# The iterative inverse carries 8 columns of N·V instead of a 64-column matrix

## The chip, the cores and the metric

The kernel runs on one core of a Trainium2 chip. The metric is the device time of one execution in microseconds (us); the time before is the median of three runs. A core has TensorE (PE in the profile, its weight loads PEld), VectorE (DVE), ScalarE (ACT), GpSimd (POOL) and SyncE (SP, the DMA queue).

## The reference, cut to what matters

The program computes two transformer-like layers over x of shape (4, 1024, 128). The change lies in the attention of layer 1, with 16 heads of 8 columns and 64 landmarks, and touches the counting of the mixture-of-experts router:

```python
def _iterative_inv(K, n_iter=6):
    I = jnp.eye(K.shape[-1], dtype=K.dtype)
    denom = jnp.max(jnp.sum(K, axis=-2), axis=-1)[..., None, None]
    V = K.swapaxes(-1, -2) / denom
    for _ in range(n_iter):
        KV = K @ V
        V = 0.25 * V @ (13.0 * I - KV @ (15.0 * I - KV @ (7.0 * I - KV)))
    return V
...
L = softmax(q @ k_l.T)            # (T, 64) of each head
P = _iterative_inv(softmax(q_l @ k_l.T))   # (64, 64)
N = softmax(q_l @ k.T)            # (64, T)
y = L @ (P @ (N @ v))             # N @ v: 64 x 8
...
oh = jax.nn.one_hot(e_ord, E)     # 2 * 4096 entries, 8 experts
cnt = take_along_axis(cumsum(oh, 0) - oh, e_ord[:, None], 1)[:, 0]
```

There are 4 x 16 = 64 heads, kept as 32 pairs: head 0 of a pair on partitions 0 to 63, head 1 on 64 to 127.

## The kernel before, in words

The program is a row of blocks, with all engines meeting between two of them: inputs of layer 0, its attention (the long part, up to about 850 us), its outputs (`layer0_outputs`), `inverse_and_routing`, `layer1_attention`, `experts`, `combine`. Within a block each engine has its own instruction list, in order, and waits on semaphores.

`layer0_outputs` loops over the four batches and leaves, for `inverse_and_routing`: KS (K after its softmax, 128 x 32 pairs x 64), NV (N·v, 128 x 32 x 8), and `oh`, the one-hot choices of the router (128 x 512). Its last instructions of a batch are the transposes of nvT on TensorE (L1207), the scaling of NV and `k_softmax` on VectorE (L968 to L971). Its GpSimd list also makes `upper` and `ones`, the left operands of the two counting products.

`inverse_and_routing` (from 987.4 us to 1098.5 us of the profiled execution) keeps A = K·V of each iteration in the left 64 columns of AQ, and Q, the product of the factors so far, in its right 64 columns. The 32 pairs are handled in NG = 4 groups of GR = 8 pairs. `squared(n, ...)` issues the products of a group: 8 pairs times 2 halves, 16 matmuls of 64 x 64 weights in fp32, each two records in the trace. A group's result of 64 columns fills one PSUM bank. TensorE's order (L1434 is the line of all of these, since the helper records them):

1. two counting products into banks 7 and 6 (L1445, L1446);
2. four column sums of K into banks 0 to 3 (L1450);
3. K transposed, four groups in banks 4 and 5 in turn, copied to X by ScalarE (L1406);
4. the Gram products K^T against itself, which give A up to the factor 1/denom;
5. six iterations of three passes of four groups: A times (7 - A), A times X, and X times AQ (128 columns, two banks a group), which gives the next A and Q at once. In the last iteration the third pass makes only Q (64 columns);
6. Q times NV (8 columns), then K^T times z (8 columns).

VectorE takes the maximum of the column sums (L1370, one instruction over four banks), its reciprocal, fills the right half of AQ with the identity over denom (L1373, 128 x 2048), scales the Gram products (L1377) and forms 7 - A (L1380); in the loop it forms 15 - and 13 - the product out of PSUM (L1387) and 7 - A of the next iteration (L1394). Between these lie small instructions for the next block: `landmarks` (L1345) and 32 memsets of `sums` (L1354). ScalarE copies the counts (L1402), the transposed K, the third pass times 0.25 (L1411, in the last iteration L1413), z (L1417), and the blocks of WM (L1426, four instructions a group).

GpSimd clears WM and `spread` and marks `spread` (L1299 to L1304), then runs the routing chain on the counts (L1311 to L1333), marks the entries and sends 32 batches of rows by indirect DMA (L1261). Each of these waits for a certain number of the groups of TensorE's loop (`i_mm`), so that they are spread over it:

```python
pool.wait_ge(sem("i_mm"), AHEAD + t * (MM * ITERS - AHEAD) // NT)   # AHEAD 12, MM 12, ITERS 6, NT 32
```

At its end GpSimd waits until all have landed.

## Time and profile before

| | us |
|---|---|
| median of three runs (lowest, highest) | 1415.3 (1413.99, 1415.97) |
| the profiled execution's own time | 1400.87 |
| its span in the trace | 1399.1 |
| TensorE busy in the span | 1265.2 (90%) |
| VectorE busy | 1009.8 (72%) |
| ScalarE busy | 864.0 (62%) |
| GpSimd busy | 236.2 (17%) |
| mean granted TensorE clock | 0.954 |

Busy shares are averages over stages with different limits; which engine sets the pace of a stage is read from that stage's rows. A granted clock of 1.00 is 2.4 GHz, 0.50 is 1.2 GHz. A name like L1434 is a line of the kernel. The instruction's line of a helper stands for all its calls, so these are told apart by the tiles and shapes behind it.

### The profile page before, as it was taken

The page shows a single profiled execution, that of the slowest core. Times are in us where ns is not written, and L with a number is a line of the kernel's source. Part 1 is how long each engine was busy: PE and PEld are TensorE (multiplying, and loading weights), DVE is VectorE, ACT ScalarE, POOL GpSimd, SP SyncE. Part 2 cuts the span into 40 slices and gives each one's busy share as a digit, 9 for nine tenths or more (in the row PEclk, how much of TensorE's full clock was granted, in tenths as well). Part 3 has the DMA queues.
Part 4 walks back from the last instruction along what each step waited for, and adds up shares of the span by engine and source line. Part 5 has one row for each costly group of instructions (what it writes and reads, how often), then busy time and mean ns, then how long its engine had stood idle before and what let it go on. Part 6 is the DMA issues. An engine that isn't in the chain of part 4 may idle for free. (4 is left out here: it accounts for less than half of the span.)

```text
span 1399.1 us, 26250 instructions
## 1 busy us (share of the span) xinstructions
PE 1265.2 (90%) x10433; PEld 595.5 (43%) x10433; DVE 1009.8 (72%) x1309; ACT 864.0 (62%) x1459; POOL 236.2 (17%) x306
## 2 busy tenths in 40 slices
PE   6967999999999999999999988898899899999990
PEld 4631222222222222222222235555699666678870
DVE  6877888898998988899899637665756388623324
ACT  3533878788887787888888855555132466543331
POOL 4200110000000000000000011100644222125560
PEclk9976999999999999999999989999999699999995
DMA  4763133331334323322120021100001111123316
GB/s 145 214 189 67 32 67 84 71 71 47 67 86 98 108 78 72 67 62 48 27 64 10 6 55 33 46 16 15 18 28 34 59 35 43 47 65 99 100 57 186
DMA packets 75206, 94.98 MB, mean 68 GB/s; under 512 B 13236, under 2 KB 44684, under 8 KB 74052
## 3 DMA queue, kind: packets, MB, share of 16 engines
q1 hardware_dynamic: 69996, 83.19, 23.6%
q0 software_dynamic: 5088, 10.12, 2.3%
q8 instruction: 82, 1.34, 0.4%
q14 instruction: 40, 0.33, 0.1%
HBM read 54.30 MB, written 38.56 MB: 66 GB/s over the span
## 5 line engine op out<-in xcount | busy, mean ns | idle before, releaser
L664 ACT ACTIVATE b_exp_ring<-psum 128x512 f32<-128x512 f32 x1024 | 555.5, 599 | 158.2 <-PE psum L719 155.0
L606 DVE TENSOR_REDUCE b_mx<-psum 128x2 f32<-128x1024 f32 x507 | 595.8, 1219 | 75.9 <-PE psum L551 74.8
L719 PE MATMUL psum<-b_q,b_k 75*128 75x512 bf16 x1024 | 311.9, 387 | 10.7 <-DMA b_q<-b_neg 9.1
L695 PE MATMUL psum<-b_exp_ring,b_v 128*32 128x512 f32 x2048 | 274.5, 608 | 0.9 <-ACT b_exp_ring L664 0.7
L719 PEld LDWEIGHTS psum<-b_q,b_k 75*128 75x128 bf16 x1024 | 79.2, 97 | 328.4 <-ACT b_exp_ring L664 223.6
L550 PE MATMUL psum<-b_k,b_q 64*128 64x512 bf16 x512 | 169.0, 395 | 25.4 <-DVE b_mx L606 10.5
L551 PE MATMUL psum<-b_ko,b_qo 64*128 64x512 bf16 x512 | 169.0, 395 | 0.0
L734 POOL CAST b_neg<-b_neg_rest 16x128 bf16<-16x128 f32 x32 | 8.9, 280 | 661.4 <-DVE b_neg_rest L617 661.4
L1835 ACT ACTIVATE e_hT<-psum,e_b 128x358 f32<-128x358 f32 (+3 forms) x96 | 53.7, 560 | 75.6 <-PE psum L1855 72.3
L550 PEld LDWEIGHTS psum<-b_k,b_q 64*128 64x128 bf16 x512 | 44.1, 93 | 127.5 <-DVE b_mx L606 41.8
L695 PEld LDWEIGHTS psum<-b_exp_ring,b_v 128*32 128x32 f32 x2048 | 41.2, 108 | 108.2 <-issue 106.4
L1261 POOL DMA_INDIRECT x_disp<-x_norm,row_sent x64 | 62.5, 976 | 122.1 <-PE psum L1633 81.4
L1765 POOL DMA_INDIRECT y_tok<-e_y,e_dest x72 | 70.8, 984 | 70.7 <-DVE e_y L1807 51.5
L1865 PE MATMUL psum<-e_w,e_hT 128*128 128x128 f32 (+1 forms) x576 | 67.4, 277 | 0.0
L1569 DVE TENSOR_REDUCE f_max<-psum 128x16 f32<-128x1024 f32 x32 | 39.2, 1225 | 37.3 <-PE psum L1633 36.5
L1865 PEld LDWEIGHTS psum<-e_w,e_hT 128*128 128x128 f32 (+1 forms) x576 | 64.6, 184 | 1.8
L1613 ACT ACTIVATE f_le<-f_lx 128x1024 f32<-128x1024 f32 x32 | 33.8, 1057 | 47.3 <-DVE f_lx L1575 47.3
L1855 PE MATMUL psum<-e_xT,e_w 128*128 128x358 f32 (+3 forms) x192 | 60.2, 468 | 0.9 <-DVE e_xT L1779 0.9
L991 DVE TENSOR_REDUCE c_nm<-psum 128x1 f32<-128x1024 f32 x32 | 37.7, 1220 | 31.7 <-PE psum L1148 31.6
L1411 ACT ACTIVATE i_aq<-psum 128x1024 f32<-128x1024 f32 x20 | 20.5, 1024 | 58.7 <-PE psum L1434 58.7
L1095 ACT ACTIVATE c_en<-psum,c_nm 128x1024 f32<-128x1024 f32 x32 | 35.7, 1117 | 32.1 <-DVE c_nm L991 32.1
L1434 PE MATMUL psum<-i_x,i_aq 64*64 64x64 f32 x1536 | 46.2, 218 | 1.4 <-DVE i_x L1380 1.4
(281 smaller groups left out, 1487.4 us busy)
## 6 DMA issues: line engine op xcount, KB each, us to landing
b_q<-q_ops SPq DMA_DIRECT2D x48, 192.0 KB
b_k<-k_ops SPq DMA_DIRECT2D x48, 192.0 KB
k_ops<-a_k SPq DMA_DIRECT2D x20, 256.0 KB, 3.2
x_disp<-b_zeros SPq DMA_DIRECT2D x13, 320.0 KB
e_x<-x_disp SPq DMA_DIRECT2D x8, 520.0 KB
v_ops<-a_vs SPq DMA_DIRECT2D x4, 1024.0 KB, 5.1
b_v<-v_ops SPq DMA_DIRECT2D x16, 256.0 KB
av_out<-b_acc SPq DMA_DIRECT2D x128, 32.0 KB, 1.7
```

What stands on the lines that cost most here:

```text
L550: g.nc.tensor.matmul(g.bank(2 * (n % 2)), q[0:MROWS, 2 * p, t], k[0:MROWS, 2 * p, keys], start=True, stop=True)
L551: return g.nc.tensor.matmul(g.bank(2 * (n % 2) + 1), qo[MROWS:P, p, t], ko[MROWS:P, p, keys], start=True, stop=True)
L606: nc.vector.reduce_max(mx[:, d % 2, :, i // 2, i % 2], pair, AX.X).then_inc(sem("b_max_done"), 1)
L664: act.activation(ex[:, n % E_RING, :], g.bank(5 + n % 3), ACT.Exp, scale=ATT_SCALE)\
L695: last = nc.tensor.matmul(AV[32 * i:32 * i + 32, :], v[s][:, at_v:at_v + 32], ex[:, (4 * group + i) % E_RING, :], start=(kb == 0), stop=(k ...
L719: nc.tensor.matmul(g.bank(5 + n % 3), k[s][0:XROWS, h, kb * P:(kb + 1) * P], q[s][0:XROWS, h, half * BANK:(half + 1) * BANK], start=True, ...
L1261: pool.indirect_dma_start(g.x_disp[:, :], bass.IndirectOffsetOnAxis(g.rows_out[:, n:n + 1], 0), g.XNW[:, n % NT, :], None).then_inc(g.sem( ...
L1434: last = nc.tensor.matmul(out[half, i, :], lhs(n * GR + i, half), rhs(n * GR + i, half), start=True, stop=True)
L1765: pool.indirect_dma_start(g.y_tok[:, :], bass.IndirectOffsetOnAxis(dest[c][0:r, t:t + 1], 0), y[c][0:r, t, :], None).then_inc(sem(f"e_sent ...
L1835: act.activation(hT[c][:, i, lo:hi], g.ps[:, (3 + n % 3) * BANK:(3 + n % 3) * BANK + hi - lo], ACT.Gelu, bias=b1[c][:, i:i + 1]).then_inc( ...
L1855: nc.tensor.matmul(g.ps[:, (3 + n % 3) * BANK:(3 + n % 3) * BANK + hi - lo], w1[c][:, i * P:(i + 1) * P], xT[:, lo:hi], start=True, stop=T ...
L1865: last = nc.tensor.matmul(g.ps[0:r, col:col + D], hT[c][:, i, t * P:t * P + r], w2[c][:, i, :], start=(i == 0), stop=(i == HC - 1))
```

## The change

It does six things. (1) Q is gone: a tile AZ holds A (64 columns) and Z (8 columns) of each pair. Z starts as NV times 1/denom, and every iteration multiplies it by its factor; the third pass has 72 columns, in the last iteration 8. All factors are polynomials in one matrix, so their order is free. The product with NV at the end is gone. (2) The two counting products move to the end of `layer0_outputs`, into banks 2 and 3, and the copies of the counts wait for nothing. (3) K's transposes come first, in four banks of their own, then the column sums; VectorE takes maximum and reciprocal for each group of pairs as its column sum comes. (4) The fills of WM, `spread` and `sums` go behind the routing chain on GpSimd, the ones in `sums` as two selections in place of 32 memsets on VectorE. (5) The dispatches' waits are spread over five iterations in place of six. (6) The blocks of WM are copied out half on ScalarE, half on VectorE.

```diff
# layer0_outputs, TensorE, after the last batch
+            chosen = g.oh[:, :, :, :].rearrange("p k n e -> p (k n e)")
+            pe.wait_ge(sem("c_kx"), B)
+            nc.tensor.matmul(g.bank(COUNTS), g.upper[:, :], chosen, start=True, stop=True).then_inc(sem("r_counts"), 1)
+            nc.tensor.matmul(g.bank(COUNTS + 1), g.ones[:, :], chosen, start=True, stop=True).then_inc(sem("r_counts"), 1)
...
# inverse_and_routing
+    ZW = LM + HD
+        AZ = sb("i_az", [P, NPAIR, ZW])
-        AQ = sb("i_aq", [P, NPAIR, P])
...
+    def landmark_block(eng_op, n, i, name):
+        w = narrow(2 * n + 1).rearrange("p (j r) d -> p j r d", r=2)
+        wm = grp(g.WM, n).rearrange("p (j r) c -> p j r c", r=2)
+        for r in range(2):
+            c = 16 * r + HD * i
+            eng_op(wm[halves[i], :, r, c:c + HD], w[halves[i], :, r, :]).then_inc(g.sem(name), 1)
...
# GpSimd: the fills stand behind the routing chain
-            nc.gpsimd.memset(g.WM[:, :, :], 0.0).then_inc(sem("i_wm"), 1)
-            nc.gpsimd.memset(g.spread[:, :, :], 0.0).then_inc(sem("f_spread"), 1)
...
+            nc.gpsimd.memset(g.WM[:, :, :], 0.0).then_inc(sem("i_wm_clear"), 1)
+            nc.gpsimd.memset(g.spread[:, :, :], 0.0).then_inc(sem("f_spread"), 1)
+            nc.gpsimd.memset(g.sums[:, :, :, :], 0.0).then_inc(sem("f_sums"), 1)
...
+            for i, half in enumerate(halves):
+                pool.wait_ge(sem("f_sums"), 1 + i)
+                to = g.sums[half, :, :, :].rearrange("p s r (t c) -> p (s r) t c", t=2)
+                nc.gpsimd.affine_select(out=to, in_=to, compare_op=ALU.not_equal, fill=1.0, base=-i,
+                                        pattern=[[-2, 2 * STEPS], [0, 2], [1, 16]], channel_multiplier=0)\
+                  .then_inc(sem("f_sums"), 1)
...
-                pool.wait_ge(sem("i_mm"), AHEAD + t * (MM * ITERS - AHEAD) // NT)
+                pool.wait_ge(sem("i_mm"), AHEAD + t * (PR * (ITERS - 1) - AHEAD) // NT)
...
# VectorE
-            link(nc.vector.reduce_max(den[:, :], g.bank(0, 4).rearrange("p (n c) -> p n c", c=LM), AX.X))
-            nc.vector.reciprocal(den[:, :], den[:, :]).then_inc(sem("i_den"), 1)
-            dve.wait_ge(sem("i_den"), 1)
-            nc.vector.tensor_tensor(AQ[:, :, LM:P], eyes[:, 3, :].unsqueeze(1).broadcast_to([P, NPAIR, LM]),
-                                    over_last(den[:, :], LM), ALU.mult).then_inc(sem("i_den"), 1)
+            for n in range(NG):
+                mine = slice(n * GR, (n + 1) * GR)
+                dve.wait_ge(sem("i_colsum"), n + 1)
+                nc.vector.reduce_max(den[:, mine], squares(n), AX.X).then_inc(sem("i_den"), 1)
+                dve.wait_ge(sem("i_den"), 2 * n + 1)
+                nc.vector.reciprocal(den[:, mine], den[:, mine]).then_inc(sem("i_den"), 1)
+            dve.wait_ge(sem("i_den"), 2 * NG)
+            nc.vector.tensor_tensor(AZ[:, :, LM:ZW], g.NV[:, :, :], over_last(den[:, :], HD), ALU.mult)\
+              .then_inc(sem("i_z0"), 1)
...
+            for n in range(NG):
+                dve.wait_ge(sem("i_landmark"), n + 1)
+                landmark_block(nc.vector.tensor_copy, n, 1, "i_wm_low")
...
# ScalarE
-                        act.activation(grp(AQ, n), both_banks(n), ACT.Copy, scale=0.25).then_inc(sem("i_aq"), 1)
+                        act.activation(grp(AZ, n), pairs_of(n)[:, :, 0:ZW], ACT.Copy, scale=0.25).then_inc(sem("i_az"), 1)
...
+                        act.activation(grp(z, n), pairs_of(n)[:, :, LM:ZW], ACT.Copy, scale=0.25).then_inc(sem("i_az"), 1)
...
# TensorE
-            nc.tensor.matmul(g.bank(7), g.upper[:, :], both, start=True, stop=True).then_inc(sem("r_counts"), 1)
-            nc.tensor.matmul(g.bank(6), g.ones[:, :], both, start=True, stop=True).then_inc(sem("r_counts"), 1)
...
+            for n in range(NG):
+                products(n, squares(4 + n), k_of, lambda p, half: g.ident[half, half], "i_kt_ps")
...
+                if n == COUNTS:
+                    pe.wait_ge(sem("r_counted"), 3)
+                nc.tensor.matmul(g.bank(n), twin[:, :], grp(g.KS, n).rearrange("p n c -> p (n c)"), start=True, stop=True)\
+                  .then_inc(sem("i_colsum"), 1)
...
+            pe.wait_ge(sem("i_z0"), 1)
...
+                cols = slice(LM if it + 1 == ITERS else 0, ZW)
                 for n in range(NG):
-                    pe.wait_ge(sem("i_x"), at(it, XS, 2 * NG + n + 1))
-                    if it + 1 < ITERS:
-                        squared(n, both_banks(n), x_of, aq_of, "i_mm")
-                    else:
-                        squared(n, both_banks(n)[:, :, LM:P], x_of, q_of, "i_mm")
+                    pe.wait_ge(sem("i_x"), at(it, PR, 2 * NG + n + 1))
+                    products(n, pairs_of(n)[:, :, cols], x_of, lambda p, half: AZ[half, p, cols], "i_mm")
             for n in range(NG):
-                pe.wait_ge(sem("i_aq"), at(ITERS - 1, AC, n + 1))
-                squared(n, narrow(2 * n), q_of, lambda p, half: g.NV[half, p, :], "i_z")
-            for n in range(NG):
-                pe.wait_ge(sem("i_z_out"), n + 1)
-                squared(n, narrow(2 * n + 1), lambda p, half: g.KS[half, p, :], lambda p, half: z[half, p, :], "i_w")
+                pe.wait_ge(sem("i_az"), at(ITERS - 1, NG, n + 1))
+                products(n, narrow(2 * n + 1), k_of, lambda p, half: z[half, p, :], "i_landmark")
```

`products` is `squared` under a new name, `pairs_of` is `both_banks`, `k_of` reads KS.

## Rows read from the trace of the kernel before

**Rows 1.** The page, its first part: busy us, share and instructions.

```profile
PE 1265.2 (90%) x10433; PEld 595.5 (43%) x10433; DVE 1009.8 (72%) x1309; ACT 864.0 (62%) x1459; POOL 236.2 (17%) x306
```

**Rows 2.** Windows: length, busy PE, PEld, DVE, ACT, POOL; clock, DMA, GB/s.

```profile
1026.60:1041.00 14.40, 14.40 (x390) 14.40 (x386) 8.43 (x22) 4.10 (x4) 6.76 (x7) 1.00 0.10 32
...
1098.50:1125.00 26.50, 20.51 (x108) 13.12 (x112) 16.32 (x20) 11.01 (x11) 7.69 (x11) 0.51 0.23 70
```

**Rows 3.** Timeline, one iteration: start, us, engine, line, what [idle before].

```profile
1012.23 7.16 PE L1434 MATMUL psum<-i_aq,i_x 64*64 64x128 f32 x128
...
1014.19 1.02 ACT L1411 ACTIVATE i_aq<-psum 128x1024 f32<-128x1024 f32 x1 [15.11 <-PE psum L1434]
...
1019.22 7.63 PE L1434 MATMUL psum<-i_x,i_aq 64*64 64x64 f32 x256
...
1026.68 7.16 PE L1434 MATMUL psum<-i_aq,i_x 64*64 64x128 f32 x128
```

**Rows 4.** Timeline, the block's start.

```profile
986.45 0.69 DVE L971 TENSOR_TENSOR k_softmax<-c_ke,c_small 128x512 f32<-128x512 f32 x1
...
987.47 1.54 PE L1445 MATMUL psum<-r_onehot,r_upper 128*128 128x512 f32 x2 [2.96 <-PEq L904]
...
990.51 4.04 PE L1450 MATMUL psum<-k_softmax,i_ones 128*128 128x512 f32 x8
...
992.25 0.19 PEld L1450 LDWEIGHTS psum<-k_softmax,i_ones 128*128 128x128 f32 x1 [0.24 <-issue]
...
994.66 2.29 DVE L1370 TENSOR_REDUCE i_den<-psum 128x32 f32<-128x2048 f32 x1 [3.66 <-PE psum L1450]
...
1000.36 0.69 DVE L1377 TENSOR_TENSOR i_aq<-psum,i_den 128x512 f32<-128x512 f32 x1
...
1006.42 1.04 DVE L1380 SCALAR_TENSOR_TENSOR i_x<-i_aq,i_eyes 128x512 f32<-128x512 f32 x1
...
1007.51 4.88 PE L1434 MATMUL psum<-i_x,i_aq 64*64 64x64 f32 x160 [0.53 <-DVE i_x L1380]
```

**Rows 5.** Timeline, the block's end.

```profile
1088.23 3.85 PE L1434 MATMUL psum<-nv,i_aq 64*64 64x8 f32 x128
...
1089.33 0.22 ACT L1417 ACTIVATE i_z<-psum 128x64 f32<-128x64 f32 x1 [0.29 <-PE psum L1434]
...
1091.93 5.45 PE L1434 MATMUL psum<-i_z,k_softmax 64*64 64x8 f32 x128
...
1097.42 0.84 ACT L1426 ACTIVATE w_landmark<-psum 64x32 f32<-64x32 f32 x4 [0.87 <-PE psum L1434]
...
1098.53 0.35 POOL L1535 MEMSET e_x<- 128x130 f32 x2 [10.75 <-POOLq L1294]
```

**Rows 6.** Groups in the block, VectorE and GpSimd: busy us, mean ns | idle before.

```profile
L1394 DVE SCALAR_TENSOR_TENSOR i_x<-i_aq,i_eyes 128x512 f32<-128x512 f32 x20 | 13.8, 692 | 24.6 <-ACT i_aq L1411 24.6
L1380 DVE SCALAR_TENSOR_TENSOR i_x<-i_aq,i_eyes 128x512 f32<-128x512 f32 x4 | 4.5, 1116 | 0.1
...
L1345 DVE SCALAR_TENSOR_TENSOR f_klm<-kl_sums,mask 128x256 f32<-128x256 f32 x4 | 1.7, 416 | 0.0
...
L1304 POOL TENSOR_SCALAR_AFFINE_SELECT f_spread<-f_spread 128x128 f32<-128x128 f32 x4 | 1.5, 410 | 0.2 <-POOL f_spread L1300 0.2
```

**Rows 7.** Timeline of GpSimd: routing chain and dispatch.

```profile
992.41 1.25 POOL L1311 TENSOR_TENSOR r_tot<-r_tot 128x504 f32<-128x504 f32 x1 [1.89 <-ACT r_tot L1402]
...
1015.12 0.24 POOL L1256 COPY x_norm<-choice_weight 128x32 f32<-128x32 f32 x1
...
1021.73 0.96 POOL L1261 DMA_INDIRECT x_disp<-x_norm,row_sent  x1 [0.30 <-issue]
```

**Rows 8.** Windows of 2 us; the clock is the third number from the right.

```profile
988.00:990.00 2.00, 2.00 (x4) 0.96 (x3) 1.74 (x7) 0.00 (x0) 1.84 (x5) 0.50 0.78 235
...
1092.00:1094.00 2.00, 2.00 (x72) 2.00 (x70) 0.00 (x0) 0.99 (x5) 0.00 (x0) 0.95 0.03 8
1094.00:1096.00 2.00, 2.00 (x42) 2.00 (x42) 0.00 (x0) 1.03 (x6) 0.00 (x0) 0.50 0.01 4
```

More of the change, by code:

```diff
@@ L158 @@
 ITERS = 6
+COUNTS = 2
 AHEAD = 12
@@ L1298, in _ @@
             link = Link(pool, sem("pool_step"), start=g.pool_steps)
-            nc.gpsimd.memset(g.WM[:, :, :], 0.0).then_inc(sem("i_wm"), 1)
-            nc.gpsimd.memset(g.spread[:, :, :], 0.0).then_inc(sem("f_spread"), 1)
-            pool.wait_ge(sem("f_spread"), 1)
-            for s in range(STEPS):
-                to = g.spread[:, s, :].rearrange("p (j h d) -> p j h d", j=4, h=HQ)
-                nc.gpsimd.affine_select(out=to, in_=to, compare_op=ALU.not_equal, fill=1.0, base=-HQ * s,
-                                        pattern=[[-32, 4], [-1, HQ], [0, HD]], channel_multiplier=1)\
-                  .then_inc(sem("f_spread"), 1)
             pool.wait_ge(sem("r_counted"), 3)
@@ L1347, in landmarks, with first @@
                   .then_inc(sem("f_klm"), 1)
-            def ones_of(s):
-                for r in range(2):
-                    for i in range(2):
-                        row = HQ * s + 2 * r + i
-                        for c in (row, 16 + row):
-                            nc.vector.memset(g.sums[LM * i:LM * i + LM, s, r, c:c + 1], 1.0).then_inc(sem("f_sums"), 1)
-            nc.vector.memset(g.sums[:, :, :, :], 0.0).then_inc(sem("f_sums"), 1)
+            def first(n):
+                nc.vector.scalar_tensor_tensor(grp(X, n), grp(AZ, n)[:, :, 0:LM], -1.0, eye(0), ALU.mult, ALU.add)\
+                  .then_inc(sem("i_x"), 1)
             nc.vector.memset(twin[:, :], 0.0).then_inc(sem("i_twin"), 1)
             dve.wait_ge(sem("i_twin"), 1)
-            dve.wait_ge(sem("f_sums"), 1)
             for half in halves:
                 nc.vector.memset(twin[half, half], 1.0).then_inc(sem("i_twin"), 1)
-            for i, f in enumerate((7.0, 15.0, 13.0, 1.0)):
+            for i, f in enumerate((7.0, 15.0, 13.0)):
                 for half in halves:
@@ L1378, in _ @@
                                         ALU.mult).then_inc(sem("i_a"), 1)
                 dve.wait_ge(sem("i_a"), n + 1)
-                nc.vector.scalar_tensor_tensor(grp(X, n), grp(AQ, n)[:, :, 0:LM], -1.0, eye(0), ALU.mult, ALU.add)\
-                  .then_inc(sem("i_x"), 1)
-            g.dve_steps = link.n
-            for it in range(0, ITERS):
+                first(n)
+            for it in range(ITERS):
                 for stage in range(2):
                     for n in range(NG):
-                        dve.wait_ge(sem("i_mm"), at(it, MM, stage * NG + n + 1))
+                        dve.wait_ge(sem("i_mm"), at(it, PR, stage * NG + n + 1))
@@ L1387, in _ @@
                         nc.vector.scalar_tensor_tensor(grp(X, n), squares(2 * n + stage), -1.0, eye(1 + stage),
                                                        ALU.mult, ALU.add).then_inc(sem("i_x"), 1)
[L1389 to L1390 removed]
+                if it < B:
+                    landmarks(it)
                 for n in range(NG if it + 1 < ITERS else 0):
[L1393 to L1395 removed]
+                    dve.wait_ge(sem("i_az"), at(it, NG, n + 1))
+                    first(n)
```

80 lines of the change are left out of this document (29 added, 51 removed).

## The prediction

> **What bounds the kernel now.** I read the page's first part, the busy shares, first: TensorE is busy 90% of the span [rows 1]. That is an average, so I went to the stretches of the block that the diff edits. In the middle of the loop TensorE is busy for all of a stretch of 14.4 us, at the full granted clock, while VectorE is busy 8.4 us and ScalarE 4.1 us of it [rows 2]. The reader is to see that TensorE alone paces the loop. The timeline of one iteration says what it pays for: four groups of the 128-column product start at 1012.23, the eight groups of 64-column products at 1019.22, the next 128-column ones at 1026.68 [rows 3]. So a 128-column group costs (1019.22 - 1012.23) / 4 = 1.747 us, a 64-column group (1026.68 - 1019.22) / 8 = 0.932 us, an iteration 14.45 us.
>
> The block's start is another stage. TensorE does counts (987.47), column sums (990.51), transposes of K and Gram products, but the first products of the loop have to wait for VectorE, which goes from the reduction (994.66) over its fill of AQ and the scaling that starts at 1000.36 to the fourth X, done at 1007.46; TensorE starts the last group of the first product at 1007.51 [rows 4]. The start is VectorE's, 20.0 us from 987.47 to 1007.51. The end of the block is a chain again: the NV product 1088.23, the K product 1091.93 to 1097.38, four ScalarE copies from 1097.42 to 1098.26 [rows 5], and the next block begins at once behind them.
>
> **The change, part by part.**
>
> *Loop, 128 to 72 columns.* Rows exist for 128 columns (1.747 us), for 64 (0.932) and for 8: the NV product's four groups take 1091.93 - 1088.23 = 3.70 us, 0.925 each [rows 5]. That 8 columns cost what 64 do says that a floor (32 weight loads and 32 matmul records a group) lies near 0.93, and that 128 columns are paced by the columns. In proportion to columns, 72 cost 1.747 x 72/128 = 0.983 us. Bounds: the floor, 0.932; and the straight line between the rows of 64 and 128, 1.034. I take 0.983, since 72 is just over the point where columns and floor meet (68). Four groups: 3.93 in place of 6.99 us, 3.06 less, five times: **15.3 us** (14.3 to 16.3). The last iteration's product goes from 64 to 8 columns, which by the rows above gives nothing.
> Cover: a group's way round is its 0.98, ScalarE's copy of 576 elements (on the line between 0.22 for 64 and 1.02 for 1024 [rows 3, 5], 0.65), VectorE's 0.69 [rows 6] and some 0.3 of handover, 2.6 us, against 4.9 us until TensorE needs that group again. VectorE needs 12 x 0.69 + 0.42 = 8.7 of 11.4 us. So TensorE stays the bound; the landmark fills (0.42 [rows 6]) and the freed 32 small memsets lie under it.
>
> *NV stage removed.* Z is carried along, so the four groups at 1088.23 go, and with them ScalarE's copies of z from their place between two products: **3.7 us**. The copy of Z group n after the last iteration (64 elements, 0.22 us [rows 5]) lies under groups n+1 to 3, and the K product of group 0 can follow on directly.
>
> *Copies of the landmark blocks.* Four ScalarE copies at the end (0.84 us [rows 5]) become two on ScalarE beside two on VectorE, which has nothing to do there: **0.4 us** (0 to 0.6). K products themselves: 5.45 us, of which the clock's part is below.
>
> *Block's start.* The two counting products (from 987.47 to the column sums at 990.51, 3.0 us) move into the outputs' end. There TensorE is done at 984.51 (987.47 less its 2.96 us of idleness) and VectorE works to 987.14 [rows 4]; at the full clock the two cost four records of 0.43 (a column sum's weight load of 0.19 behind 0.24 of idleness, at the full clock [rows 4]), 1.7 us, so they end at 986.3 and VectorE still ends the block. At half clock it would be 3.4 us, ending at 988.0: up to 0.9 us lost. I take 0. Then the new order: K transposes from 987.47, four groups of 64 columns, 3.73 [rows 3]; column sums, eight records, 3.4, to 994.6. ScalarE copies the counts meanwhile (three copies of 512 elements, 0.6 each by the line above, done by 989.3) and frees the two banks long before column sum 2. VectorE reduces each group as it comes, so only the last reduction is left (512 elements, 0.69 as the multiplication of that size at 986.45 [rows 4]), a reciprocal (0.2, an estimate: the smallest instructions here take 0.22 [rows 5]), and Z0 over 256 elements, 0.42 by the landmark fill of that size [rows 6], 0.3 more for handovers: ready at 996.2. Before, it came to this point at 1000.36. The first Gram product (from 994.6, 0.93) lies ahead of it. Then the same eight VectorE instructions as before, which took 1000.36 to 1007.46, 7.1 us: fourth X at 1003.3, last group starts at 1003.4. **4.1 us** less.
> Bounds: the X instructions took 1.12 us here and 0.69 in the loop, with the same shape [rows 6]; GpSimd was in its routing chain beside the former, and only sent rows beside the latter. The chain will start about 3 us earlier (its first instruction is at 992.41, released by the copies of the counts, its last at 1015.12 [rows 7]) but with 23 us it still covers 996 to 1003, so I keep 1.12. Without that neighbour four instructions would save 1.7 more: 5.8. Below: if the clock is low for the first 3.5 us, as it was at 988 to 990 [rows 8], two groups at double price are 1.8 us lost: 2.3.
> The Trainium skill, "SBUF — State Buffer", section "SBUF: two separate sides", says that VectorE (with two SBUF inputs) and a GpSimd instruction that reads SBUF lock each other out of a shared port pair for a whole instruction. The rows agree, since the subtraction of AQ and eyes reads SBUF twice (1.12), while the scaling out of PSUM stays at 0.69. By that rule Z0, with two SBUF inputs, may wait a GpSimd instruction as well, and the sum would be about 1 us less.
>
> *GpSimd.* The fills of WM, spread and sums move behind the routing chain: three memsets and six selections, of which four take 0.41 for 128 elements [rows 6]; the others are of 256 to 1,024 elements, and I count 0.7 for each of those five, 5 us in all (an estimate). Chain from 989.3 plus 23.0 plus 5: dispatches start at 1017.3. They are 32, at 0.96 + 0.30 = 1.26 us back to back [rows 7], so 1058. The waits now want product 58 at the latest, which is at about 1056. The block will end near 1075, and DMA landing has 17 us. Before, GpSimd sat 10.75 us between its last dispatch and the next block [rows 5]. Cost 0; the cover is those 17 us. SP's queue: the two query loads keep their place.
>
> Sum: 15.3 + 3.7 + 0.4 + 4.1 = **23.5 us**. The profiled execution took 1400.9 us (span 1399.1), the median of the runs is 1415.3, so 14.4 us lie between an execution with and without the profiler; I carry the difference over unchanged: 1415.3 - 23.5 = **1391.8 us** (profiled: 1377.4).
>
> **The clock.** TensorE's granted clock is 1.00 (2.4 GHz) up to 1092, 0.95 in the next 2 us and 0.50 (1.2 GHz) from 1094 [rows 8], in the middle of products of 8 columns that came without a gap; it stays there to about 1125 in the next block [rows 2]. In the changed kernel the run of 8-column products is as long (last iteration's in place of NV's, then K's), so I leave the fall where it is. If it doesn't come, the K products cost 3.7, and 1.7 us are won; in the next block's low stretch TensorE is busy 20.5 of 26.5 us [rows 2], and a fall or rise that comes some us sooner or later moves the time by part of that; I allow 2 us either way for it.
> The Trainium skill, "TensorE: Matmul & The Clock Gate", section "What's actually happening", has the clock fall to half after idleness. The rows show it falling while TensorE is recorded as busy all the time, so for this place I go by the rows. By the page there would be no fall here, and the gain would be 25.2 us.
>
> **Rivals.**
> (a) *Clock falls inside the loop* (ends slower). 8 columns brought it down [rows 8]; the loop now carries fewer columns. Against it: eight groups of 64 columns, 7.46 us in a row, five times, leave it at 1.00 [rows 2, 3], and 72 is more than 64. Price: groups double at most, 0.93 to 1.86; it decides from 24 us of the 65 us loop on; all of it low would be 65 - 23.5 = 42 us slower, 1457. Chance 4%.
> (b) *The way round, not TensorE, sets the loop*: GpSimd's fills and dispatches slow VectorE's X (1.12 for 0.69), or a wide group waits for its bank. The three VectorE passes of an iteration would need 12 x 1.12 = 13.4 us, 2 us over 11.4, but GpSimd's SBUF-reading work ends with the second iteration and eight of the twelve read PSUM: at most 2 iterations, 4 us lost: 1396. If it held throughout, 10 us lost: 1402. Chance 10% for 1396 to 1405.
> (c) *Gain stays, routing now ends the block*: it decides from 17 us on by which GpSimd or its DMAs end later than I think, and 40 us later the gain is all gone: 1415. Nothing speaks for it but the missing landing times. Chance 3%.
> (d) *Forecast*, 83%, of it (e) low clock at the block's start, 1.8 us less, 1393.6, a third.
>
> **How the numbers follow.** The bounds add to 14.3 + 3.7 + 0 + 2.3 - 0.9 = 19.4 and 16.3 + 3.7 + 0.6 + 5.8 + 1.7 = 28.1 us, with the next block's clock a few us more on either side: 1385 to 1398 holds the forecast and the nearer half of (b). Faster by over 0.2% (2.8 us, about what a measurement of this kernel can tell): 0.83 + 0.10 = 0.93; within: 0.03 from (c); slower: 0.04 from (a).
>
> **What the profile will show.** The 72-column groups start 0.98 us apart, and iterations 11.4 us (0.93 and 11.2, or 1.03 and 11.6, are my bounds). The first loop product's last group starts 15.9 us behind the block's start. No product reads NV in this block. VectorE's X of the first pass costs 1.1 us each. GpSimd's dispatches run back to back and end about 17 us ahead of the block. A PEclk row under 0.9 between the first and last 72-column product, a VectorE wait that TensorE sits behind in later iterations, or an outputs' block that ends later than VectorE's last multiplication would make me wrong.

## The result, and the profile after

The changed kernel takes 1403.7 us (median of 4 runs, 1401.9 to 1405.3), the kernel before 1415.6 beside it (4 runs, 1414.0 to 1418.0): ratio 0.9922, 95% interval 0.9901 to 0.9943. It is faster, by 11.9 us where 23.5 were forecast, and its time is 5.7 us above the range of 1385 to 1398. The profiled execution took 1402.7 us, its span 1400.7: no 14 us lie between the two this time.

The page's first part answers to [rows 1]. TensorE is recorded as busy 5.8 us less, where 15.3 + 3.7 us of its work were to go:

```profile
PE 1259.4 (90%) x10305; PEld 584.6 (42%) x10305; DVE 1008.6 (72%) x1288; ACT 851.2 (61%) x1447; POOL 236.5 (17%) x309
```

The windows next, one iteration in the middle of the loop and then the last one (columns as in [rows 2]):

```profile
1046.30:1061.10 14.80, 13.36 (x384) 12.37 (x385) 8.38 (x13) 2.49 (x4) 7.88 (x8) 1.00 0.13 39
...
1076.20:1087.35 11.15, 11.15 (x390) 11.15 (x387) 6.64 (x10) 1.65 (x5) 0.00 (x0) 1.00 0.02 7
```

An iteration was to take 11.4 us and takes 14.8. In [rows 2] TensorE was busy for 14.40 of 14.40 us; here it is idle for 1.44 of 14.80, at the full clock. In the last iteration, where GpSimd does nothing (0.00), TensorE is busy throughout, and does as many matmuls (390) in 11.15 us as in the middle (384) in 14.80. So the loss is larger than the recorded idleness. The waits between 1031 and 1076 us (who, for whom: us in total, times, longest) say what the idleness waits for:

```profile
POOL x_disp L1266 <- PE psum L1442: 21.6, 25, 1.2
DVE i_x L1404 <- PE psum L1442: 13.2, 15, 1.0
PEld psum L1442 <- issue: 7.1, 18, 0.5
...
PE psum L1442 <- issue: 4.5, 13, 0.4
```

In the last two rows TensorE waits for nothing that the profile shows ("issue"); no engine's result is what it lacks. I read this as instructions that come late, which is an argument so far. VectorE and GpSimd wait for TensorE, not the reverse. The timeline shows beside what:

```profile
1018.41 1.15 POOL L1266 DMA_INDIRECT x_disp<-x_norm,row_sent  x1 [0.57 <-POOL x_norm L1261]
...
1019.87 0.96 POOL L1266 DMA_INDIRECT x_disp<-x_norm,row_sent  x1 [0.30 <-issue]
1020.40 0.39 PE L1442 MATMUL psum<-i_x,i_az 64*64 64x64 f32 x6 [0.33 <-issue]
...
1021.13 0.36 PE L1442 MATMUL psum<-i_x,i_az 64*64 64x64 f32 x5 [0.34 <-issue]
1021.14 0.96 POOL L1266 DMA_INDIRECT x_disp<-x_norm,row_sent  x1 [0.30 <-issue]
...
1035.22 3.35 PE L1442 MATMUL psum<-i_x,i_az 64*64 64x64 f32 x97 [0.39 <-issue]
...
1036.00 0.96 POOL L1266 DMA_INDIRECT x_disp<-x_norm,row_sent  x1 [1.16 <-PE psum L1442]
...
1076.21 7.66 PE L1442 MATMUL psum<-i_x,i_az 64*64 64x64 f32 x256
...
1083.67 3.88 PE L1442 MATMUL psum<-i_az,i_x 64*64 64x8 f32 x128
...
1087.38 5.84 PE L1442 MATMUL psum<-i_z,k_softmax 64*64 64x8 f32 x128
...
1093.84 0.35 POOL L1526 MEMSET e_x<- 128x130 f32 x2 [18.29 <-POOLq L1308]
```

TensorE runs in short pieces of 5 or 6 matmuls while GpSimd sends rows back to back, and in unbroken stretches of 128 and 256 once the sends are over. The last row but one is K's product, the last GpSimd's first work in the next block.

The block's start, also from the timeline, beside [rows 4]:

```profile
987.29 1.02 PE L1218 MATMUL psum<-r_onehot,r_ones 128*128 128x512 f32 x2
988.54 0.69 DVE L972 TENSOR_TENSOR k_softmax<-c_ke,c_small 128x512 f32<-128x512 f32 x1
989.56 3.95 PE L1442 MATMUL psum<-ident,k_softmax 64*64 64x64 f32 x128 [1.24 <-PEq L905]
...
993.43 3.70 PE L1456 MATMUL psum<-k_softmax,i_ones 128*128 128x512 f32 x8
...
998.14 0.55 DVE L1391 TENSOR_TENSOR i_az<-nv,i_den 128x256 f32<-128x256 f32 x1
...
1004.65 1.05 DVE L1373 SCALAR_TENSOR_TENSOR i_x<-i_az,i_eyes 128x512 f32<-128x512 f32 x1
1005.75 4.88 PE L1442 MATMUL psum<-i_x,i_az 64*64 64x64 f32 x160 [0.53 <-DVE i_x L1373]
```

The counting products end at 988.31, before VectorE's last multiplication does (989.23). Counted from the K transposes (989.56), the column sums end after 7.6 us (forecast 7.1), Z0 is ready after 9.1 (8.7), and the last group starts after 16.2 (15.9).

The traces are compared below by five stages, cut at VectorE's instructions: *start* (from the memset of i_ones, with which the block begins, to the end of the fourth X), *loop* (from the start of the first X multiplication that reads a product to that of the last, 48 of them), *tail* (from there to the first maximum of attention, f_max), *attention* (first to last of its 32 maxima), and *rest* (to the end of the span).

| us | start | loop | tail | attention | rest |
|---|---|---|---|---|---|
| before, the trace of the rows | 19.7 | 77.3 | 15.4 | 110.3 | 188.7 |
| changed | 16.1 | 78.3 | 11.5 | 112.4 | 192.9 |

Read so, the loop has got longer, and so have two stages that the diff doesn't touch. That was the first riddle.

### The profile page after: what moved, and what is told of

Read it like the earlier page. It is cut to its first block and busy times, and to the rows that moved or that the text cites. A ratio compares the mean times of both kernels' runs of the same rounds, so it can differ in the third digit from the quotient of the medians.

```text
span 1400.7 us, 25966 instructions
## 1 busy us (share of the span) xinstructions
PE 1259.4 (90%) x10305; PEld 584.6 (42%) x10305; DVE 1008.6 (72%) x1288; ACT 851.2 (61%) x1447; POOL 236.5 (17%) x309
## 3 DMA queue, kind: packets, MB, share of 16 engines
q1 hardware_dynamic: 69996, 83.19, 23.4%
## 5 line engine op out<-in xcount | busy, mean ns | idle before, releaser
L1442 PE MATMUL psum<-i_x,i_az 64*64 64x64 f32 x1536 | 53.1, 222 | 6.3 <-issue 4.5
L1428 ACT ACTIVATE i_az<-psum 128x576 f32<-128x576 f32 x20 | 12.6, 650 | 70.5 <-PE psum L1442 70.5
## 6 DMA issues: line engine op xcount, KB each, us to landing
b_q<-q_ops SPq DMA_DIRECT2D x48, 192.0 KB
b_k<-k_ops SPq DMA_DIRECT2D x48, 192.0 KB
```

The source lines that it names most:

```text
L1442: last = nc.tensor.matmul(out[half, i, :], lhs(n * GR + i, half), rhs(n * GR + i, half), start=True, stop=True)
```

## Experiments

Eighteen runs were made, in six sessions, each session on one chip with the kernel before beside it; the first and the fourth fell on the same chip, so five chips took part. Theory S ("theory A" in the expectations): GpSimd's indirect sends hold up TensorE's supply of instructions, and narrow products leave no reserve against that. Rivals: W, it is GpSimd's waits for TensorE's products; D, it is the data that the sends move; N (near "theory B"), the 72-column form is itself slower than I forecast. A last one, I, stands in the expectation of a2: the 16 KB loads of instructions cause the gaps.

### First session: kernel before; padded; sends moved

*a0* is the kernel before. *a1* pads the passes of 72 columns to 128 with zeros:

```diff
-        AZ = sb("i_az", [P, NPAIR, ZW])
+        AZ = sb("i_az", [P, NPAIR, P])
...
+            nc.gpsimd.memset(AZ[:, :, ZW:P], 0.0).then_inc(sem("i_pad"), 1)
...
-                cols = slice(LM if it + 1 == ITERS else 0, ZW)
+                cols = slice(LM, ZW) if it + 1 == ITERS else slice(0, P)
```

*a2* sends nothing in the loop, and two blocks of 128 rows in each tile of attention (the marking of the entries moves to the middle of attention with them):

```diff
-            for t in range(NT):
-                pool.wait_ge(sem("i_mm"), AHEAD + t * (PR * (ITERS - 1) - AHEAD) // NT)
-                dispatch(g, pool, t)
-            pool.wait_ge(sem("dispatched"), 16 * NT)
...
             for n in range(NT):
                 pool.wait_ge(sem("f_scores"), n + 1)
-                dispatch(g, pool, NT + n)
+                dispatch(g, pool, 2 * n)
+                dispatch(g, pool, 2 * n + 1)
```

*a3* is a2 with the 32 waits kept, each before a memset of one column in place of the send.

> The kernel before, unchanged, profiled beside the others, because its profiled execution of the first session took 1400.9 us and its timed runs 1414 to 1418. If the two belong to two chips or sessions, this execution takes about 1415 us and its trace says which block has the 14 us. If the profiler makes it faster, it takes 1401 again. In the block of the inverse both theories expect iterations of 14.45 us and no gap over 0.1 us in TensorE's starts of 64-column products.

> The changed kernel with a third pass of 128 columns again (56 of them zeros; ScalarE still copies 72, Z still has 8). Theory A, TensorE's instruction supply: a 64-column group uses its instructions as fast as they come (29 ns each), each indirect send of GpSimd holds the supply up for about half a microsecond, and the wide pass used to let the queue fill again. Then iterations with sends take 14.45 us here, no longer than the 14.75 us of the changed kernel, with no gaps, and the whole is within 3 us of the changed kernel, rather faster. Theory B, columns: the gaps of the changed kernel have another cause (the fills of GpSimd, the layout of AZ), which stays, and 3.06 us a pass come on top: iterations of 17.8 us, 15 us slower.

> The changed kernel with all 64 sends in the attention block, two a tile, none in the loop. Theory A: all five iterations take 11.2 to 11.4 us as the last one does, the loop is 17 to 20 us shorter, the attention block gets some us longer if the sends hold TensorE up there too; net 10 to 19 us faster than the changed kernel, about 1388. Theory B: the gaps stay, nothing is gained. A third theory, instruction loads: the 16 KB loads alone cause the gaps; they stay too.

> As a2_sends_in_attention, but GpSimd keeps the 32 waits on the loop's products, with a memset of one column behind each in place of the send. If the send itself holds up TensorE (theory A), iterations take 11.2 to 11.4 us as in a2. If it is the waiting on TensorE's semaphore, they take 14.7 us as in the changed kernel.

Measured: the kernel before took 1399.8 us here, not 1415 (13 runs); a0 1401.8 (ratio 1.0003, 0.9984 to 1.0022), a1 1392.1 (0.9934, 0.9910 to 0.9957), a2 1376.9 (0.9833, 0.9805 to 0.9861), a3 1379.7 (0.9850, 0.9817 to 0.9883). a0's profiled execution took 1406.0 us with a span of 1404.2. So an execution with the profiler isn't 14 us shorter than one without: there are chips on which the kernel before takes 1400 us, and others on which it takes 1415. The trace of the rows came from one of the former, the timed runs from one of the latter. On this chip iterations of 128 columns took 14.45 us with the sends in them, as in the rows, and a2's and a3's 11.47. The 14.45 us that I had expected of a1 came, and of a2 and a3 about the 11.2 to 11.4. But nothing held TensorE up here, so a1 to a3 can't tell S, W and D apart.

### Second session: changed again; before again; before with sends moved; 96 columns

*b0* is the changed kernel, *b1* the one before. *b2* is the kernel before with a2's edit; *b3* is a1 with 96 in place of 128.

> The changed kernel, unchanged, beside the others. Its first profile had iterations of 14.7 us with gaps in TensorE's starts and 3.54 us a tile in the attention, where every other trace has 3.45; the kernel before was timed at 1415 in that session and at 1400 in the last one. If theory A holds for the kernel (narrow passes leave no reserve, each send costs 0.41 us), the gaps are here again and it is about 16 us slower than the version with the sends in the attention, 1390 to 1393 if before is at 1400. If the gaps belonged to that session's chip, iterations take 11.5 us here and it is at 1376 to 1380.

> The kernel before, once more, for its trace on the chip of these runs: 14.45 us an iteration, 3.45 us a tile, 1397 to 1406 in all if the chip is like the last one. What differs between executions should lie ahead of the changed block.

> The kernel before with all 64 sends in the attention block. Theory A: its wide passes hid the sends already, so its iterations stay at 14.45 us and the whole stays within 2 us. So the gain of the changed kernel with the same move would be the change's own, not the move's. If the sends cost TensorE time in the kernel before too, this one is some us faster.

> The changed kernel with a third pass of 96 columns (24 of them zeros). Columns alone: 4 x 1.747 x 96/128 = 5.24 and 7.46 for the other two passes, 12.7 us an iteration. Theory A in numbers: supply for an iteration takes 12 x 0.93 = 11.2 us, eight sends 8 x 0.41 = 3.3 us, 14.5 us together, whichever is more: so 14.5 to 14.75 us again, and a time within 2 us of the changed kernel.

Measured, with the kernel before at 1413.4 us (19 runs): b0 1399.6 (0.9900, 0.9884 to 0.9917), b1 1415.0 (1.0002, 0.9987 to 1.0018), b2 1413.8 (1.0004, 0.9990 to 1.0019), b3 1402.6 (0.9918, 0.9899 to 0.9937). The windows show that the kernel before is held up on this chip too; b1, the same length in the middle of the loop:

```profile
1040.00:1054.80 14.80, 14.38 (x354) 13.84 (x349) 7.77 (x20) 4.10 (x4) 5.76 (x6) 1.00 0.10 30
```

TensorE is idle 0.42 us there, where [rows 2] has none, and it gets through fewer matmuls: 354 in 14.8 us, against 390 in 14.4. b1's loop is 82.9 us. Without sends (b2) it is back at 77.3, and attention grows from 112.9 to 118.4, so the time stays. I had expected b1 like the first session's chip (14.45 us an iteration; it has about 15.5), b3's iterations at 14.5 to 14.75 us and its time within 2 us of b0's. They are 15.35 us and it is 3.0 us slower: the padding isn't free, and a sum of a fixed price a send on top of a floor doesn't give it.

### Third session: changed; sends moved; plain copies; sends later

*c0* is the changed kernel, *c1* is a2. *c2* leaves the first 32 indirect sends out, so half the routed rows never arrive; SyncE copies the same rows to a spare place in DRAM, behind the same products:

```diff
+            for t in range(NT):
+                sp.wait_ge(sem("i_mm"), AHEAD + t * (PR * (ITERS - 1) - AHEAD) // NT)
+                sp.dma_start(spare_rows[t, :, :], g.XNW[:, t, :]).then_inc(sem("plain"), 16)
```

*c3* sends later, over the whole loop:

```diff
-                pool.wait_ge(sem("i_mm"), AHEAD + t * (PR * (ITERS - 1) - AHEAD) // NT)
+                pool.wait_ge(sem("i_mm"), 20 + t * (PR * ITERS - 20) // NT)
```

> So far the kernel before ran at 1400 with no gaps and 3.45 us a tile of the attention on some chips (kind I: its first profile, the four kernels of the first call), and at 1414 with gaps at the sends and 3.54 us a tile on others (kind II: its first timed runs, the changed kernel's two profiles, the second call). If this call falls on kind I (before near 1400), theory A with the kinds expects iterations of 11.47 us, no gaps, and 1376 to 1379, the forecast's 23 us. If on kind II (before near 1414), again 14.7 us an iteration and 1399 to 1404. A theory in which the sends cost TensorE time in this kernel on every chip expects gaps on kind I too.

> The changed kernel with all sends in the attention, two a tile, which had 11.47 us an iteration and 3.45 us a tile on kind I. On kind II: iterations of 11.47 us (16 us less than the changed kernel there) but tiles of 3.85 us in place of 3.54 (31 tiles, 9.6 us more), so 5 to 8 us faster than the changed kernel. On kind I: the same time as the changed kernel within 2 us.

> The first 32 indirect sends of GpSimd are left out (half of the routed rows never arrive), and SyncE copies as many rows of the same size to a spare place in their stead, at the same products of the loop. On kind II: if it is the data moved that holds TensorE up, the gaps and the 14.7 us stay; if it is GpSimd's making of the descriptors, iterations take 11.5 us. On kind I no gaps in either.

> The changed kernel with the sends from product 20 on and spread to the end of the sixth iteration, 1.6 products apart, so that GpSimd never has three to catch up with. On kind II: no run of gaps at the start, the clock stays at 1.00, the first full iteration loses its extra 3 us and the sum of the others stays (32 times 0.4 us): 2 to 4 us faster than the changed kernel. On kind I no difference.

Measured, before at 1413.7 us (7 runs): c0 1399.7 (0.9897, 0.9877 to 0.9916), c1 1392.8 (0.9857, 0.9832 to 0.9882), c2 1383.8 (two runs; 0.9786, 0.9761 to 0.9812), c3 1399.4 (0.9903, 0.9881 to 0.9925). The windows of the same 14.8 us in the middle of the loop, for c0:

```profile
1040.00:1054.80 14.80, 13.17 (x383) 12.12 (x380) 8.24 (x13) 2.49 (x4) 7.88 (x8) 1.00 0.13 38
```

for c1:

```profile
1040.00:1054.80 14.80, 14.80 (x498) 14.80 (x496) 10.24 (x17) 3.91 (x6) 0.00 (x0) 1.00 0.02 4
```

and for c2:

```profile
1040.00:1054.80 14.80, 14.80 (x501) 14.80 (x498) 10.31 (x17) 3.26 (x5) 0.00 (x0) 1.00 0.18 50
```

With the eight sends (c0) TensorE does 383 matmuls and is idle 1.63 us; without them about 500 and is never idle. c2 moves more data than c0 in this stretch (50 GB/s against 38), and nothing is lost: theory D falls, and N with it, since c1's and c2's iterations are 11.47 us on this chip as well. Theory I falls too: the loops of c0, c1 and d0 have 17 loads of instructions each, and only c0's has gaps.

The gaps also lie at a fixed distance from the send. The last send of c0's loop, and TensorE's next weight load behind a gap:

```profile
1074.05 0.96 POOL L1266 DMA_INDIRECT x_disp<-x_norm,row_sent  x1 [0.72 <-PE psum L1442]
...
1075.41 0.26 PEld L1442 LDWEIGHTS psum<-i_az,i_x 64*64 64x64 f32 x6 [0.51 <-issue]
```

The load starts 1.36 us behind the send's start. For all of the last 26 sends of this loop it is 1.31 to 1.39 us, though GpSimd waited 0.5 to 1.5 us before them, and no product is waited for behind the last one. This speaks against W, as do the two sends at 1019.87 and 1021.14 in the profile after, which waited for no product ("issue") and have the densest gaps. The tiles of attention's maxima in c1 show where a part of the gain goes back:

```profile
L1559 DVE TENSOR_REDUCE f_max<-psum x32: 1224/1225/1226, 1075.2 to 1194.8; 128x16 f32<-128x1024 f32 x32
```

and in c0:

```profile
L1560 DVE TENSOR_REDUCE f_max<-psum x32: 1224/1225/1226, 1095.9 to 1206.4; 128x16 f32<-128x1024 f32 x32
```

119.6 us with two sends a tile, 110.5 with one: 9.1 us for 32 sends, 0.28 each; by b1 and b2 it was 5.5 us, 0.17 each. Both kernels have the same wait per tile there, so in attention it is the second send and not the wait. (On the first session's chip the same edit takes attention from 109.3, d0 below, to 109.8.) c3 was to be 2 to 4 us faster than c0 and is 0.3. Its clock stays at 1.00 in the loop, as expected, and its loop is 4.3 us shorter than c0's (75.0), but its tail is 1.9 and its attention 2.5 longer: next to nothing is won.

### Fourth session: changed; 128 columns

*d0* is the changed kernel and *d1* is a1.

> The changed kernel once more, to catch a chip of kind I. If before is near 1400 (kind I): 11.47 us an iteration, no gaps, 3.45 us a tile, 1375 to 1380 by theory A with kinds; 1386 or more and gaps if narrow passes make the sends costly on every chip. If before is near 1414 (kind II): 14.7 to 15.1 us, as in three profiles so far.

> The changed kernel with a third pass of 128 columns, which on kind I took 14.45 us an iteration with no gaps and told nothing of the sends. On kind II: the kernel before takes 15.5 us an iteration there with 6.4 sends, the pass of 96 columns 15.35 with 8. If width only buys reserve against the sends: 15.4 to 15.9 us, within 6 us of the changed kernel (15 by columns alone). On kind I: as before, 1390 to 1393.

It ran on the chip of the first session. Before took 1402.1 us (12 runs), d0 1378.7 (0.9829, 0.9800 to 0.9858), d1 1395.4 (0.9946, 0.9925 to 0.9968). Here the changed kernel, with the same sends behind the same products, gains what was forecast: 23.4 us. (d1 was expected at 1390 to 1393 and is 2 us above; a1, the same kernel on this chip, took 1392.1.) d0's window of 14.8 us in the loop:

```profile
1040.00:1054.80 14.80, 14.80 (x505) 14.80 (x503) 11.18 (x18) 3.31 (x6) 11.45 (x12) 1.00 0.17 54
```

Twelve sends (GpSimd busy 11.45 us) and TensorE never idle. Its timeline, a send in the middle of an unbroken stretch of 128 matmuls:

```profile
1024.71 4.17 PE L1442 MATMUL psum<-i_az,i_x 64*64 64x72 f32 x128
...
1025.19 0.96 POOL L1266 DMA_INDIRECT x_disp<-x_norm,row_sent  x1 [0.30 <-PE psum L1442]
...
1028.71 3.49 PE L1442 MATMUL psum<-i_x,i_az 64*64 64x64 f32 x114
```

### Fifth session: 128 columns; half the sends

*e0* is a1 again, *e1* keeps 16 of the 32 sends in the loop, three products apart, and puts 48 into attention:

```diff
-            for t in range(NT):
-                pool.wait_ge(sem("i_mm"), AHEAD + t * (PR * (ITERS - 1) - AHEAD) // NT)
+            for t in range(NT // 2):
+                pool.wait_ge(sem("i_mm"), AHEAD + 2 * t * (PR * (ITERS - 1) - AHEAD) // NT)
                 dispatch(g, pool, t)
```

> The changed kernel with a third pass of 128 columns, third try for a chip of kind II (before near 1414). There: 15.4 to 15.9 us an iteration, since the kernel before takes 15.5 with 6.4 sends an iteration and this one has 8; the loop no more than 3 to 6 us longer than the changed kernel's 79, where columns alone ask for 15. On kind I: 14.45 and no gaps, as twice before.

> The changed kernel with 16 sends in the loop, 3 products apart, and 48 in the attention (one a tile in its first half, two in its second). If each send costs the narrow loop 0.4 to 0.5 us on kind II, the loop takes 62.4 + 16 x 0.45 = 69.6 us there (78 to 79 with 32 sends, 62.4 with none), and the attention lies between its 110.5 to 112.4 and its 119.5. Net within 4 us of the version with all sends in the attention. On kind I: 62.4 us and no difference.

Before 1414.4 us (9 runs), e0 1407.8 (0.9954, 0.9929 to 0.9978), e1 1393.9 (0.9852, 0.9829 to 0.9876). Both iterations missed what I expected: e0's are 16.5 us (I had 15.4 to 15.9), e1's 12.2, with a loop of 66.4 (I had 69.6). Its ratio of 0.9852 is that of c1 (0.9857), within 4 us as expected. A send's price is no constant.

### Sixth session: waits alone; sends alone

*f0* is a3 again; *f1* has the changed kernel's sends back to back behind a single wait:

```diff
-                pool.wait_ge(sem("i_mm"), AHEAD + t * (PR * (ITERS - 1) - AHEAD) // NT)
+                if t == 0:
+                    pool.wait_ge(sem("i_mm"), AHEAD)
```

> The changed kernel with the 32 sends of the loop moved into attention, and their 32 waits for TensorE's products kept in the loop, each followed by a one-column memset. It tells something only on a chip where the kernel before takes 1412 us or more. If the send holds TensorE up, the loop (first to last X multiplication that reads a product) is 62.4 us, iterations 11.47, and the time that of the kernel with all sends in attention, 0.9857 of the kernel before (0.983 to 0.988). If GpSimd's wait holds it up, iterations stay near 14.8 and the loop at 78, and the ratio is 1.00 to 0.995. On a chip where the kernel before takes about 1400 us both theories give 62.4 and 0.985.

> The changed kernel, its 32 sends back to back behind one wait for the twelfth product, 1.26 us apart, some 40 us in all. If the send holds TensorE up, by 0.42 to 0.6 us each, the loop is 62.4 + 32 x 0.5 = 78 us (76 to 82), all of it in the first 40 to 45 us and the last iteration clean at 11.5; ratio 0.988 to 0.993. If the wait holds it up, one wait is left, the loop is 63 us and the ratio 0.979. On a chip where the kernel before takes about 1400 us the loop is 62.4 by both and the ratio 0.983.

The chip was a fifth one, and of the kind without gaps: before 1402.5 us (7 runs), f0 1379.1 (0.9827, 0.9788 to 0.9866), f1 1378.1 (0.9821, 0.9781 to 0.9862), both loops 62.4 us. It separates nothing, but shows how complete the absence is: in f1 GpSimd sends 32 times within 42 us and TensorE's iterations stay at 11.47.

### What the sessions show together

Kind I are the chips of sessions 1 and 4 (one chip) and 6, and the trace of the rows; kind II those of sessions 2, 3 and 5 (three chips), the first timed runs and the first runs of the changed kernel. No session mixed them. Stages, of one trace each:

| us | kind | start | loop | tail | attention | rest |
|---|---|---|---|---|---|---|
| before (a0) | I | 19.8 | 77.3 | 15.6 | 110.1 | 189.6 |
| changed (d0) | I | 16.1 | 62.4 | 12.1 | 109.3 | 189.1 |
| 128 columns (a1) | I | 16.2 | 77.3 | 13.5 | 109.3 | 188.6 |
| sends in attention (a2) | I | 16.1 | 62.4 | 11.8 | 109.8 | 189.0 |
| before (b1) | II | 20.1 | 82.9 | 18.6 | 112.9 | 193.7 |
| before, sends moved (b2) | II | 19.4 | 77.3 | 17.8 | 118.4 | 191.8 |
| changed (c0) | II | 16.1 | 79.4 | 12.5 | 110.5 | 192.9 |
| 96 columns (b3) | II | 16.1 | 80.4 | 13.3 | 112.1 | 192.9 |
| 128 columns (e0) | II | 16.2 | 85.8 | 11.6 | 112.2 | 193.1 |
| sends in attention (c1) | II | 16.1 | 62.4 | 11.9 | 119.5 | 194.6 |
| half the sends (e1) | II | 16.1 | 66.4 | 12.9 | 116.4 | 192.0 |

What lies ahead of these stages is left out of the table: the block starts between 983.6 and 992.4 us in these traces, whatever the kernel, so differences of a few us between single executions say little, and the medians decide.

The price of a send on kind II, from a steady iteration less the same iteration of kind I (or without sends), over the sends in it: 72 columns, eight sends, (14.8 - 11.47) / 8 = 0.42 us; 96 columns, (15.35 - 12.7) / 8 = 0.33, where the 12.7 is 11.47 and the 1.28 us by which b3's first iteration, which has no send in it, is longer than c0's; 128 columns, (16.5 - 14.45) / 8 = 0.26; 72 columns, four sends, (12.2 - 11.47) / 4 = 0.18. The kernel before, 128 columns with 6.4 sends, gives about (15.5 - 14.45) / 6.4 = 0.16. By c0 instead of the first profile the first price is 0.45. A gap in TensorE's weight loads is at most some 0.5 us long. Wider products hide more of it, and so does more room between sends. The gaps are all of the loss: the stretches of over 0.2 us between the starts of two weight loads add up, over the loop, to 16.4 us in c0, 12.2 in b3, 8.7 in e0, 6.1 in b1 and 4.1 in e1, and these loops are 17.0, 11.6, 8.5, 5.6 and 4.0 us longer than the same without gaps (for b3 by the estimate of its iteration). No loop of kind I, and none without sends on kind II, has one such stretch. That TensorE's instructions are fetched ahead, and wide products give the fetching time to get ahead again, would explain the prices; it is argued from these numbers, and no run shows the fetching.

## Why the prediction was right and wrong

*The step that failed* is the sentence "Cost 0" of the part on GpSimd, and with it "So TensorE stays the bound". I checked when the sends would end, what they wait for and what they delay downstream; I didn't ask whether they cost the engine beside them anything. In the trace of the rows they don't: it is of kind I. On kind II the sends were already worth 5.6 us of the loop before (82.9 against 77.3, b1 and b2), and in the changed kernel 15.9 to 17.0 (78.3 to 79.4 against 62.4). So the term "15.3" for the loop is worth 82.9 - 78.3 = 4.6 us, or 3.5 by c0. The 32 sends are the same; they fall eight to an iteration instead of 6.4, on narrower products. The 10.7 us that the term lacks are most of the 11.6 us that the whole missed.

*What should have warned me* is the other failed sentence: "14.4 us lie between an execution with and without the profiler; I carry the difference over unchanged". Profiled executions took 1.7 to 2.1 us more than their spans and agree with the unprofiled runs of their session (1402.7 and 1403.7 for the changed kernel, 1406.0 among 1396.6 to 1406.0 for a0). The 14.4 us were the difference between two kinds of chip: of the 16.4 us between the spans of b1 and of the rows' trace, 9.2 lie in the block (121.6 and 112.3), 2.5 in attention and 5.0 in the rest, with 0.4 the other way ahead of the block. A difference that sits in the stages can't be carried over; a term may change with it, and here the largest did.

The other terms on kind II, b0 against b1 on one chip: start 4.0 us for 4.1, tail 6.9 for 4.1, attention and rest 0.7 and 0.9 that weren't forecast. The tail's surplus is mostly the clock's: in b1 and b2 it fell already in the NV products, and K's products took 7.0 us instead of 5.45. So start, loop and tail make 15.4 us there, of which a part is this accident, and all stages 17.0; the medians of the session give 13.8.

*Where the mechanism was as forecast,* the sizes by kind I (d0 against the trace of the rows):

- Loop: 77.3 - 62.4 = 14.9 us for 15.3. An iteration takes 11.47 us and a 72-column group (11.47 - 7.46) / 4 = 1.003 us for 0.983, between the bounds 0.932 and 1.034.
- Start: 19.7 - 16.1 = 3.6 us for 4.1. The column sums ended 0.4 us late and Z0 took 0.55 for 0.42; the four X instructions took 0.87 to 1.52, in the mean 1.12 as taken. Z0's excess is 0.13 us beside GpSimd's chain, whose instructions there take 1.0 us. By the port rule of the Trainium skill's "SBUF — State Buffer" ("SBUF: two separate sides") Z0 might have waited for a whole instruction of GpSimd; this trace shows no such wait.
- NV stage and copies: 3.7 + 0.4 = 4.1 us, measured in the tail 15.4 - 12.1 = 3.3. K's product takes 5.84 us or more instead of 5.45, since the clock fell earlier in it (d0: 6.37 us, with 0.76 in the window in which it starts, where [rows 8] has 0.95).
- Counting products: they cost nothing in the outputs' end; VectorE's last multiplication ends 0.9 us behind them.
- GpSimd idle before the next block: 17.7 us for 17, with the dispatches back to back as forecast; on kind II it is 18.3, and there they wait for TensorE.
- The way round of a group was compared with 4.9 us until TensorE needs it again. Four groups of 0.98 us lie between, so it is 3.9; the 2.6 us still fit in.

Together the block gains 112.3 - 90.5 = 21.8 us and attention 1.1, 22.9 for 23.5 forecast and 23.4 measured.

*The rivals.* None of them names what happened. The measured 1403.7 lies among (b)'s 1396 to 1405, but by accident: (b) has VectorE late, and VectorE waits for TensorE. (c) didn't come: GpSimd is done early. (e), the low clock at the block's start, didn't come: start is 16.1 us in every trace of the changed kernel. (a), a fall of the clock in the loop, came once and briefly in each of the three traces of the changed kernel on kind II, behind its first sends. The windows of 2 us in the first of them:

```profile
1020.00:1022.00 2.00, 0.97 (x18) 0.69 (x16) 0.12 (x1) 0.00 (x0) 1.70 (x2) 1.00 0.21 67
1022.00:1024.00 2.00, 0.95 (x15) 0.55 (x13) 0.57 (x1) 0.00 (x0) 1.05 (x2) 0.99 0.15 52
1024.00:1026.00 2.00, 1.94 (x36) 1.94 (x38) 0.82 (x2) 0.00 (x0) 0.96 (x1) 0.50 0.05 15
1026.00:1028.00 2.00, 2.00 (x50) 2.00 (x48) 1.05 (x2) 0.00 (x0) 0.96 (x1) 0.65 0.20 65
...
1088.00:1090.00 2.00, 2.00 (x57) 2.00 (x55) 0.46 (x4) 0.43 (x4) 0.00 (x0) 0.71 0.04 12
```

TensorE ran 0.97 and then 0.95 of 2.00 us, and the granted clock went from 0.99 to 0.50 (2.4 to 1.2 GHz); at 1028 us it was back at 1.00. With the sends back to back it makes the second iteration long, 17.7 us against 14.8 for the next, 3 us of the loss; b3, whose clock didn't fall there, has 16.5 against 15.35, so more than a third of the 3 us may be the bunched sends alone. "TensorE: Matmul & The Clock Gate" of the Trainium skill ("What's actually happening") has the clock fall to half after idleness. This fall agrees in so far as the engine was idle for about half of the time before it. The last row is the other kind of fall, in K's products: at 0.71 with TensorE recorded busy 2.00 of 2.00 us. In [rows 8] it came at 1092 to 1094.

## What stays open

What in a chip makes it of kind I or II. Whether in the loop it is the send alone: the runs with waits or sends alone (a3, f0, f1) all fell on kind I. For the send speak attention, where the waits are the same and only the sends double (c0 and c1, b1 and b2), c2, where another engine's waits for the same products cost nothing, and the gaps' fixed distance from the send (c0). GpSimd's own waits without sends on kind II weren't seen. By which path a send holds TensorE up: not by the data (c2), and in c0 the gap ends 1.3 to 1.4 us behind the send's start, about 0.2 us before its own packets start at 1.53; more the traces don't show.

## What to carry to other kernels

When a profiled execution and the timed runs differ by more than their own scatter, they can come from two machines and not from one with a correction, as here (1400.9 and 1415.3 us): find the stages in which they differ before any row is used as a price. A free engine that issues many indirect transfers can cost the bound engine time, and the narrower that engine's instructions are made, the more of it is seen; put such transfers where they cost less, or far apart, and measure. With the sends in attention instead of the loop the changed kernel is 6.9 us faster on kind II (1392.8 for 1399.7) and the same on kind I (ratios to before 0.9833 and 0.9829); the kernel before gains nothing by it (1413.8 for 1413.4).

## What the runs showed of the hardware

- GpSimd's indirect sends of 128 rows came with gaps of up to some 0.5 us in TensorE's weight loads on three of the five chips of the sessions, at a price of 0.16 to 0.45 us a send by the width of the products and the distance of the sends; on two there was none (0 stretches of over 0.2 us in d0, 32 in c0). The kernel before took 1400 to 1403 us on these two and 1413 to 1415 us on those three.
- A plain DMA of the same rows, issued by SyncE, cost TensorE nothing (501 matmuls in 14.8 us, 498 without any).
- Sixteen products of 64x64 by 8 or 64 columns take 0.93 us; by 72, 1.003; by 128, 1.747.
- The granted clock went from 0.99 to 0.50 behind 4 us in which TensorE was recorded busy for 1.92, and fell also under unbroken products of 8 columns ([rows 8]).
